# Self-attention by pairs of steps: narrow blocks share a pair of score banks, wide blocks are mirrored

## The reference, cut to what matters

```python
scores = jnp.einsum('bhid,bhjd->bhij', q, k)
rel = jnp.einsum('bhid,pd->bhip', q, rel_key)
rel_idx = jnp.clip(j - i + p - 1, 0, p - 1)
bias = jnp.take_along_axis(rel, rel_idx, axis=3)
logits = jnp.where(j <= i, (scores + bias) * scale, -jnp.inf)
out = jnp.einsum('bhij,bhjd->bhid', softmax(logits), v)
```

## Time and profile before

| what | value |
|---|---|
| median of 3 runs | 498.36 us (495.96 to 498.57) |
| profiled execution | 497.16 us |
| its span in the profile | 495.4 us |
| mean granted TensorE clock | 0.976 of 2.4 GHz |
| self-attention steps in the span | from 36.9 us to 338.6 us |

### The profile page before, as it was taken

How to read it: one execution, slowest core, us unless ns; L and a number is a source line. 1 busy time by engine, 2 the same in 40 slices (tenths; PEclk the granted TensorE clock), 3 DMA queues, 4 the chain that set the end, 5 groups by cost and what they waited for, 6 DMA issues and landing times.

```text
span 495.4 us, 17255 instructions
## 1 busy us (share of the span) xinstructions
PE 449.7 (91%) x7304; PEld 274.2 (55%) x7304; DVE 335.2 (68%) x684; ACT 267.2 (54%) x811; POOL 162.0 (33%) x95
## 2 busy tenths in 40 slices
PE   0879999999999799999799999998898989999997
PEld 0554655655655555655565665564454434666765
DVE  5555886657977667885857887766667587466633
ACT  2546556756456446556535655554454556554653
POOL 7147383333350952360752422084300000001000
PEclk9999999999999799999889999999889899999999
DMA  8211000000100000000000000000000004503151
GB/s 287 66 70 46 26 3 24 24 18 8 26 24 1 24 10 17 26 24 2 24 3 24 3 3 3 3 4 2 2 0 1 1 0 172 171 23 141 53 176 38
DMA packets 17465, 19.49 MB, mean 39 GB/s; under 512 B 1659, under 2 KB 14575, under 8 KB 17263
## 3 DMA queue, kind: packets, MB, share of 16 engines
q1 hardware_dynamic: 17391, 18.41, 11.5%
HBM read 16.17 MB, written 2.16 MB: 37 GB/s over the span
## 4 chain that ended last, share of the span: by engine, by line
PE 70%; DVE 17%; issue 5%; ACT 5%; DMA 2%; POOL 1%; DVEq 0%; SPq 0%; ACTq 0%; POOLq 0%
PE psT L1432 15%; PE psS L1403 14%; PE psS L1413 8%; PE psOM L1372 8%; PE psT L1792 5%; PE psS L1775 4%; DVE neg_max L1058 3%; DVE x_max L1033 2%; PE psS L1622 2%; PE psOM L1513 2%; ACT prob L663 2%; PE psT L1513 2%; PE psOM L1649 1%; DVE prob L1278 1%; PE psOM L1460 1%
## 5 line engine op out<-in xcount | busy, mean ns | idle before, releaser
L663 ACT ACTIVATE prob<-psS,neg_max 128x208 f32<-128x208 f32 (+23 forms) x256 | 121.2, 479 | 74.3 <-DVE neg_max L1058 74.1
L1058 DVE TENSOR_REDUCE neg_max<-psS 128x2 f32<-128x672 f32 (+23 forms) x128 | 91.7, 717 | 64.8 <-PE psS L1413 63.8
L445 POOL TENSOR_TENSOR stat<-stat,pack_a_sb 128x4 f32<-128x4 f32 (+2 forms) x16 | 54.7, 3416 | 169.9 <-DVE stat L876 123.0
L1432 PE MATMUL psT<-pack_a_sb,prob 128*128 128x128 f32 (+4 forms) x640 | 99.2, 287 | 6.3 <-DVE pt_even L1014 3.3
L1432 PEld LDWEIGHTS psT<-pack_a_sb,prob 128*128 128x128 f32 (+4 forms) x640 | 65.1, 133 | 48.5 <-issue 31.4
L1403 PE MATMUL psS<-k_v,q_both 64*32 64x336 f32 (+23 forms) x2048 | 88.5, 403 | 2.6 <-ACT prob L663 1.3
L1413 PE MATMUL psS<-rel_shifted,q_both 36*32 36x268 f32 (+16 forms) x2048 | 71.8, 338 | 0.0
L479 POOL TENSOR_TENSOR q_both<-qT,pack_a_sb 128x1024 f32<-128x1024 f32 x16 | 31.6, 1973 | 85.4 <-PE psS L1413 82.9
L1413 PEld LDWEIGHTS psS<-rel_shifted,q_both 36*32 36x32 f32 x2048 | 37.4, 110 | 24.7 <-issue 17.5
L663 ACT ACTIVATION_READ_ACCUMULATOR prob<-psS,neg_max 128x1 f32 x256 | 50.5, 197 | 0.0
L1792 PEld LDWEIGHTS psT<-pack_b_sb,prob 128*128 128x128 f32 x288 | 36.1, 191 | 18.6 <-DVE prob L1278 11.7
(11 more groups left out here) (172 smaller groups left out, 597.7 us busy)
## 6 DMA issues: line engine op xcount, KB each, us to landing
q_rep<-q_scratch SPq DMA_DIRECT2D x128, 32.0 KB
k_v<-w_scratch SPq DMA_DIRECT2D x8, 512.0 KB, 5.9
q_both<-w_scratch SPq DMA_DIRECT2D x8, 512.0 KB, 6.6
pack_b_sb<-pack_b_dram SPq DMA_DIRECT2D x1, 1641.5 KB, 9.7
X<-x_dram SPq DMA_DIRECT2D x4, 256.0 KB, 5.3
q_scratch<-qT SPq DMA_DIRECT2D x4, 256.0 KB, 2.0
out_dram<-X SPq DMA_DIRECT2D x4, 256.0 KB, 2.3
pack_a_sb<-pack_a_dram SPq DMA_DIRECT2D x1, 535.0 KB, 4.4
```

Of the source, the lines that this page charges most:

```text
L445: nc.gpsimd.tensor_tensor(st[:, 5, 0:groups], st[:, 2, 0:groups], ca["root"][0:parts, 0:groups], ALU.pow).then_inc(seeded, 1)
L663: ins = nc.scalar.activation(prob[:, s % 4, half, 0:wide], psS[:, 2 * (s % 2) + half, 0:wide], ACT.Exp, bias=neg_max[:, s % 2, half:half + 1],
L1058: v.tensor_reduce(neg_max[:, s % 2], psS[:, 2 * (s % 2):2 * (s % 2) + 2, 0:wide], AX_X, ALU.max, negate=True).then_inc(max_ready, 1)
L1432: ins = nc.tensor.transpose(psT[0:w, k % 2, at:at + T], prob[:, s % 4, half, j * T:j * T + w], ident)
```

## The change

Narrow blocks: from step 2 on, two steps make a pair. Both write one pair of banks, the even step at columns 0 and on, the odd one at 256 and on, and the next pair uses the other pair of banks. The even step reads as many keys as the odd one (`read_width`). TensorE does S, S, T, T, A, A of the pair in the even step; one VectorE instruction takes the maxima of both steps, then come both steps' copies; ScalarE does both exponentials in its even step. Extras stay in the steps where they were, behind the pair's work, so those of the odd step follow those of the even one.

Wide blocks from g = 2 on, steps 2 to 5: an even step does S, T, A, A, an odd one T, S, so that two S stand together and two A. VectorE copies ahead of the maximum in the odd steps. `neg_max` has four slots instead of two.

The new functions:

```diff
+        def in_pair(g, u):
+            return ORDER[g % TB] < 2 and u >= 2
+        def read_width(g, u):
+            return width(ORDER[g % TB], u | 1 if in_pair(g, u) else u)
+        def bank_at(s):
+            g, u = divmod(s, BS)
+            return 2 * (fill_of[s] % 2), 256 * (u % 2) if in_pair(g, u) else 0
+        def mirrored(g, u):
+            return g > 0 and ORDER[g % TB] >= 2 and 2 <= u <= 5
```

ScalarE's loop (`exponentials` holds what stood in it):

```diff
             for s in range(ALL_STEPS):
                 if s >= 2:
                     copy_units(s - 2)
-                act.wait_ge(max_ready, s + 1)
...
+                if not in_pair(g, u):
+                    exponentials(s)
+                elif u % 2 == 0:
+                    exponentials(s)
+                    exponentials(s + 1)
                 if g and u == 5:
                     copy_inverses(g - 1)
```

VectorE's instruction for a pair, and its loop:

```diff
+            def maxima_of_pair(s):
+                bank, at = bank_at(s)
+                dve.wait_ge(scores_ready, s + 2)
+                v.tensor_reduce(neg_max[:, s % 4:s % 4 + 2, :].rearrange("p s b -> p b s"),
+                                psS[:, bank:bank + 2, :].rearrange("p b (s j) -> p b s j", s=2)
+                                [:, :, :, 0:read_width(*divmod(s, BS))],
+                                AX_X, ALU.max, negate=True).then_inc(max_ready, 1)
...
-                if s >= 2:
+                if mirrored(g, u) and u % 2:
                     copy_units(s - 2)
+                    maxima(s)
+                elif not in_pair(g, u):
+                    maxima(s)
+                    if s >= 2:
+                        copy_units(s - 2)
+                elif u % 2 == 0:
+                    maxima_of_pair(s)
+                    copy_units(s - 2)
+                    copy_units(s - 1)
```

TensorE's wait in `scores`, and its loop:

```diff
-                pe.wait_ge(scores_read, PRO + s - 1)
+                if fill_of[s] > 1:
+                    pe.wait_ge(scores_read, PRO + first_step[fill_of[s] - 1])
...
-                scores(s)
-                if s >= 2:
+                if mirrored(g, u):
+                    if u % 2:
+                        transpose_weights(s - 2)
+                        scores(s)
+                    else:
+                        scores(s)
+                        transpose_weights(s - 2)
+                        attend_block(g - 1, u - 2)
+                        attend_block(g - 1, u - 1)
+                elif not in_pair(g, u):
+                    scores(s)
+                    if s >= 2:
+                        transpose_weights(s - 2)
+                    if g and 2 <= u <= 5:
+                        attend_block(g - 1, u - 2)
+                elif u % 2 == 0:
+                    scores(s)
+                    scores(s + 1)
                     transpose_weights(s - 2)
-                if g and 2 <= u <= 5:
-                    attend_block(g - 1, u - 2)
+                    transpose_weights(s - 1)
+                    if u <= 5:
+                        attend_block(g - 1, u - 2)
+                        attend_block(g - 1, u - 1)
```

More of the change, by code:

```diff
@@ L111, in build @@
         x_key1 = sb("x_key1", [128, H * M])
-        neg_max = sb("neg_max", [128, 2, 2])
+        neg_max = sb("neg_max", [128, 4, 2])
         row_sum = sb("row_sum", [128, 2, 2 * BS])
@@ L258, in width, with pair_of_banks @@
             return (blk * BS + (5 if u in (2, 3) else u + 1)) * QG
+        def in_pair(g, u):
+            return ORDER[g % TB] < 2 and u >= 2
+        def read_width(g, u):
+            return width(ORDER[g % TB], u | 1 if in_pair(g, u) else u)
+        def pair_of_banks():
+            fills, firsts = [], []
+            for s in range(ALL_STEPS):
+                g, u = divmod(s, BS)
+                if not (in_pair(g, u) and u % 2):
+                    firsts.append(s)
+                fills.append(len(firsts) - 1)
+            return fills, firsts
+        fill_of, first_step = pair_of_banks()
+        def bank_at(s):
+            g, u = divmod(s, BS)
+            return 2 * (fill_of[s] % 2), 256 * (u % 2) if in_pair(g, u) else 0
+        def mirrored(g, u):
+            return g > 0 and ORDER[g % TB] >= 2 and 2 <= u <= 5
         def units(blk):
@@ L649, in copy_heads_tile, with exponentials @@
                                      ACT.Identity, scale=cb["ln_g"], bias=cb["q_b"]).then_inc(piece_read, 1)
-            for s in range(ALL_STEPS):
+            def exponentials(s):
                 g, u = divmod(s, BS)
-                b, n = divmod(g, TB)
-                wide = width(ORDER[n], u)
-                if s >= 2:
-                    copy_units(s - 2)
-                act.wait_ge(max_ready, s + 1)
+                wide = width(ORDER[g % TB], u)
+                bank, at = bank_at(s)
+                act.wait_ge(max_ready, fill_of[s] + 1)
                 if s >= 4:
@@ L662, in _ @@
                 for half in range(2):
-                    ins = nc.scalar.activation(prob[:, s % 4, half, 0:wide], psS[:, 2 * (s % 2) + half, 0:wide],
-                                               ACT.Exp, bias=neg_max[:, s % 2, half:half + 1],
+                    ins = nc.scalar.activation(prob[:, s % 4, half, 0:wide], psS[:, bank + half, at:at + wide],
+                                               ACT.Exp, bias=neg_max[:, s % 4, half:half + 1],
                                                accum_out=row_sum[:, g % 2, 2 * u + half:2 * u + half + 1])
                 ins.then_inc(scores_read, 1)
+            for s in range(ALL_STEPS):
+                g, u = divmod(s, BS)
+                b, n = divmod(g, TB)
+                if s >= 2:
[5 more added lines that the diff above has]
+                    exponentials(s + 1)
                 if g and u == 5:
@@ L1044, in x_shift, with maxima @@
                                 ALU.add).then_inc(x_shift_read, 1)
+            def maxima(s):
+                bank, at = bank_at(s)
+                dve.wait_ge(scores_ready, s + 1)
+                v.tensor_reduce(neg_max[:, s % 4], psS[:, bank:bank + 2, 0:read_width(*divmod(s, BS))],
+                                AX_X, ALU.max, negate=True).then_inc(max_ready, 1)
+            def maxima_of_pair(s):
+                bank, at = bank_at(s)
+                dve.wait_ge(scores_ready, s + 2)
+                v.tensor_reduce(neg_max[:, s % 4:s % 4 + 2, :].rearrange("p s b -> p b s"),
+                                psS[:, bank:bank + 2, :].rearrange("p b (s j) -> p b s j", s=2)
+                                [:, :, :, 0:read_width(*divmod(s, BS))],
+                                AX_X, ALU.max, negate=True).then_inc(max_ready, 1)
             for s in range(ALL_STEPS):
                 g, u = divmod(s, BS)
-                wide = width(ORDER[g % TB], u)
                 if g and u == 2:
@@ L1391, in scores @@
                 blk = ORDER[n]
-                wide = width(blk, u)
+                wide = read_width(g, u)
+                bank, at = bank_at(s)
                 if u == 0:
@@ L1402, in scores @@
                         rows = slice(HALF_ROWS * half, HALF_ROWS * (half + 1))
-                        mm(psS[32 * c:32 * c + 32, 2 * (s % 2) + half, 0:wide],
+                        mm(psS[32 * c:32 * c + 32, bank + half, at:at + wide],
                            q_blk[rows, g % 2, q0:q0 + QT, :].rearrange("p i h -> p (i h)"),
@@ L1412, in scores @@
                         rows = slice(HALF_ROWS * half, HALF_ROWS * half + QT * HD + QT)
-                        ins = mm(psS[32 * c:32 * c + 32, 2 * (s % 2) + half, lo:wide],
+                        ins = mm(psS[32 * c:32 * c + 32, bank + half, at + lo:at + wide],
                                  q_rel[rows, g % 2, q0:q0 + QT, :].rearrange("p i h -> p (i h)"),
```

6 lines of the change are left out of this document (2 added, 4 removed).

## The result

Both kernels were timed on one chip: the changed one takes **540.93 us** (median of 4, 540.5 to 542.46), the kernel before 498.36 (495.96 to 498.57). The ratio is 1.088, with a 95% interval of 1.084 to 1.092: slower, as forecast, but by 42.6 us and not by 21, and above the range of 503 to 528. The profiled execution took 541.34, its span is 539.6, 44.2 more than before; the mean granted clock is 0.940 against 0.976.

A forecast was written before the change was run, and what follows sets the result against it. TensorE bounds the kernel, with 70% of the chain that ended last. 497.16 - 11.4 saved + 14.6 (blocks 5, 9, 13) + 3.7 (other narrow) + 5.9 (wide) + 9.3 (clock) = 519.3, said as 519 us; range 503 to 528.

The forecast's parts named there:

- TensorE's saving: Fewer changes of work kind on TensorE in narrow pairs and mirrored wide blocks: -11.4 us together.
- Blocks 5, 9 and 13: Longer TensorE waits around the layer norm, the tokens piece, `project_o` and the heads' pieces: +14.6 us.
- From there to the end of refine's first instruction 2.37: Block 5's chain: from the end of ln_sum to the end of refine's first instruction, root on GpSimd included, 2.37 us.
- To the piece 136.58 - 135.20 = 1.4: Block 5's chain: from the end of refine's first instruction to the tokens piece, 1.4 us.
- The heads' piece of blocks 9 and 13: The second piece of steps 2 and 3 waits for the first's copy behind E(2) and E(3): 1.0 us each.
- `project_o` behind E(6), E(7) and the copy: In blocks 5, 9 and 13 `project_o` waits for both exponentials and the piece's copy: 3.3 us.
- Wide blocks: T(5) and, in each block 2, T(1) wait for VectorE's copies; hidden in g = 6 and 10: +5.9 us.
- The clock: Granted clock falls to 0.50 after the new waits of blocks 5, 9 and 13: 3 x 3.1 = +9.3 us.
- Other narrow blocks: New waits in block 3 (+2), block 11 (+1), blocks 1 and 7 (+0.7 together): +3.7 us.
- the one on the longer side: Clock also falls in block 3 and after wide waits, or changes of tile save nothing: 526 to 531; 12%.

The follow-up runs named there:

- the first experiment: The changed kernel with GpSimd made to wait for the layer norm's multiply before its next work in blocks 5, 9 and 13: 526.66 us, ratio 1.059.
- experiment 6: The changed kernel, GpSimd behind the norm and ScalarE's tokens-piece copy ahead of E(6) and E(7) in blocks 5, 9, 13: 504.07 us.
- Experiment 8: The kernel before with the mirrored order in wide blocks alone, no pairs: 508.98 us, ratio 1.022.
- Experiment 12: The kernel before with the mirrored order in steps 2 and 3 of wide blocks only, no pairs: 497.41 us, ratio 1.000.
- experiment 11: The changed kernel with the norm's multiply as four products of 128x128 in place of one product of two tiles: 544.66 us, ratio 1.094.
- experiment 5: The changed kernel with idle transposes that nobody reads filling TensorE's waits in blocks 5, 9 and 13: 535.61 us, ratio 1.078.

## Why the forecast was half of what came

- **TensorE's saving: right.** In block 5, two S, two units of T and two weighted pieces in a row, and then single ones of before:

```profile
130.18 0.58 PE L1471 MATMUL psS<-k_v,q_both 64*32 64x208 f32 x16
...
130.91 0.56 PE L1471 MATMUL psS<-k_v,q_both 64*32 64x208 f32 x16
...
131.76 1.09 PE L1500 MATMUL psT<-pack_a_sb,prob 128*128 128x128 f32 x8
132.78 0.65 PE L1437 MATMUL psOM<-pt_even,V_now 128*32 128x128 f32 x16
...
134.23 0.61 PE L1471 MATMUL psS<-k_v,q_both 64*32 64x224 f32 x16
```

```profile
128.70 0.64 PE L1372 MATMUL psOM<-pt_even,V_now 128*32 128x128 f32 x16
...
129.50 0.58 PE L1403 MATMUL psS<-k_v,q_both 64*32 64x208 f32 x16
...
130.95 0.64 PE L1372 MATMUL psOM<-pt_even,V_now 128*32 128x128 f32 x16
```

  The first S takes 130.91 - 130.18 = 0.73, a single one of as many columns 130.36 - 129.50 = 0.86 (T(2) starts at 130.36). T T takes 1.02, two single ones 2 x (130.95 - 130.36) = 1.18; A A 1.45 against 2 x (129.50 - 128.70) = 1.60. That is 0.13, 0.16 and 0.15, where 0.15, 0.10 and 0.14 were forecast. Block 1, which has no such extras, is 1.20 shorter.
- **Blocks 5, 9 and 13: the step that failed.** "From there to the end of refine's first instruction 2.37 ... To the piece 136.58 - 135.20 = 1.4" took over durations of before, and with them GpSimd's place. The forecast named what VectorE has ahead of the norm; it did not ask what else S(7), moved ahead, releases. After, from the start of refine's first instruction to the end of the multiply it is 148.89 - 140.49 = 8.4 us, in the first experiment 1.3. In block 13, where GpSimd masks no keys, refine is as long, the multiply is not held, and the wait is 5.35 instead of 7.41. The kernel before had shown the signature once: refine's first instruction took 0.79 and ended at 135.20, within 0.02 of the end of GpSimd's preparation of tokens, and the next two took 0.16 each:

```profile
133.88 1.30 POOL L470 TENSOR_TENSOR X<-X,pack_b_sb 128x512 f32<-128x512 f32 x1
...
135.24 0.16 DVE L835 TENSOR_TENSOR stat<-stat 128x4 f32<-128x4 f32 x1
135.44 0.16 DVE L836 SCALAR_TENSOR_TENSOR stat<-stat 128x4 f32<-128x4 f32 x1
```

  I had used the 0.79 and not asked for its cause. The rest of the chain was rather too long: with GpSimd away, the three blocks lost 7.5 us, not 11.8. The 2.37 held both that hold and work that stood beside the root; in experiment 1 the same distance, from the end of `ln_sum` (138.39, where the idle time of 1.13 begins) to 139.68, is 1.3. The heads' piece of blocks 9 and 13 waits 0.8, forecast 1.0.
- **`project_o` behind E(6), E(7) and the copy: right.** It waits 2.7 us after the piece (1.8 in block 13), forecast 3.3; put ahead of the exponentials, the copy costs 0.47 (experiment 6).
- **Wide blocks: the chain was right, who stands behind it was not.** Only T(5), and T(1) in block 2 of an element, were asked after. Experiment 8 shows the probe (1.0, in blocks 10 and 14) and the heads' piece (0.6, in 8 and 12) of step 6 waiting for `finish` or `copy_inverses`. In blocks 6 and 10 I let the wait hide at the end; block 6, where T(5) waits 0.80 and S(7) 0.47 for the exponentials of E(5), is 0.94 longer, and the first two steps of block 7 give back 0.19 of that. From S(2) to S(6) block 10 does save 0.54, as forecast (0.58); it is lost again at step 6. Experiment 12 shows the loss to be that of steps 4 and 5.
- **The clock: near in size, partly by luck.** The steps behind blocks 5, 9 and 13 took 8.2 us more, forecast 9.3; counted as in experiment 1, the whole span took 11.4 more. But experiment 1, whose waits are nearer to the forecast's, took 14.1 more, so the size does not follow from the waits alone. The clock also fell behind block 3, and of the time at 0.50 in block 5, 145 to 159, about half is the wait itself, where it costs nothing.
- **Other narrow blocks: about right.** `project_o` of block 3 waits 2.0 for the key piece's copy where it waited 0.3, forecast 2 more. Block 11 is 0.85 longer, forecast 0.1, and a fall of the clock behind block 3 (+1.19) was not counted.
- **Of the rivals** the one on the longer side came nearest, but for another reason: neither block 3's clock alone nor a missing saving, but GpSimd, which the forecast had only for the root.

On these turns of VectorE and GpSimd the Trainium skill, "SBUF — State Buffer", section "Who interferes with whom", says that VectorE and GpSimd share one pair of ports, that whoever holds it keeps it for the whole instruction, and that a VectorE instruction with two inputs in SBUF contends with a GpSimd instruction that reads SBUF. The traces agree: 1.88 and 2.46 us where 0.16 is the length alone. The same section lists VectorE's `tensor_scalar`, the form of experiment 11, among those that can take both ports and so can contend. By that rule the four products could be held, and they were, 2.84 us against 0.88.

## What to carry to other kernels

When an instruction moves, ask which engines wait for its semaphore, not only for what it computes: the work that it releases moves too, and may land beside something that was alone. An instruction that takes five times its usual length is a row to explain before its number is used in a sum. When a chain gets later, list everything that stands behind it in program order, and take the first, not the one that waits today.

## What the runs showed of the hardware that was not expected

- GpSimd doesn't slow down in these turns (1.97, 2.55 and 2.28 us beside the norm; 1.97, 2.57 and 2.27 in the kernel before, where the norm was over); VectorE does, by up to 2.3 us for an instruction of 0.16. VectorE's copies from PSUM are not held: 0.42 at 142.05 beside GpSimd's product at 142.10 in experiment 1.
- Transposes of a unit matrix that nobody reads kept the granted clock at 1.00 through waits of 7.4 and 2.7 us (experiment 5), although TensorE still idled 2.23 and 1.14 us of those of block 5.
